# Cross-attention on one core: Wv turned by DMA, a V projection and three Wo slices moved into the first iteration, a stack fill cut in two

## The chip, the core and the metric

The kernel runs on one core of a Trainium2 chip. A core has TensorE (PE in the rows; its weight loads are PEld), VectorE (DVE), ScalarE (ACT), GpSimd (POOL) and SyncE (SP), which issues all DMAs of this kernel from one queue, in order. The metric is device time in microseconds (us), the median over runs.

## The reference

Eight batches; x is 224 x 512 and the context 750 x 512 in each, 16 heads of 32.

```python
q = (x @ Wq.T + bq).reshape(B, Nq, 16, 32).transpose(0, 2, 1, 3)
k = (ctx @ Wk.T + bk).reshape(B, Nk, 16, 32).transpose(0, 2, 1, 3)
v = (ctx @ Wv.T + bv).reshape(B, Nk, 16, 32).transpose(0, 2, 1, 3)
att = softmax(einsum('bhqd,bhkd->bhqk', q, k) / sqrt(32))
out = einsum('bhqk,bhkd->bhqd', att, v).transpose(0, 2, 1, 3).reshape(B, Nq, 512)
out = x + out @ Wo.T + bo
out = (out - mean) / sqrt(var + 1e-5) * gamma + beta
```

## The kernel before

All operands of the large matmuls are split into two f16 parts, a high one (ScalarE) and a low one (VectorE), and a product is three matmuls (high-high, high-low, low-high). Weights and tokens are needed with the 512 input features on the partitions, so they are turned.

**Prologue.** A list of tasks (`prologue`) is run in order by TensorE, each into one of six PSUM banks: four that later hold scores, two that later hold tasks. `("W", "v", 2)` turns 128 rows of Wv by four 128 x 128 transposes; ScalarE and VectorE then write its two parts into `wT`. `("ctxT", i)` and `("xT", i)` turn tokens. `("K", g, half)`, `("Q", g)` and `("V", i)` are projections: K for 128 features and half of the keys, Q for 128 features, V for 125 keys and all features. Their outputs go to `parts` (K, Q) or `v`.

**Iterations.** Each batch is an iteration of 32 steps: four units (of four heads), eight steps each. Step s issues the row scores of step s + 1 (L605), whose row maxima VectorE takes (L911) before the next unit needs them. The unit before is worked on in the same steps: key-major scores (L629), the exponential on ScalarE (L792), sums over keys on GpSimd (L1019 to L1027); the product with V (L645) follows two units behind. Projections are spread over the steps by tables: `OWN` for what this batch still lacks, `NEXT` for the next batch (`("Q", 0)` of the next batch stands at step 24), `OUTPUT` for the output projection of the batch before, steps 18 and 20. Steps 18 and 20 of iteration 0 are empty, as are steps 1 and 9 in it. The tasks use two PSUM banks in turn, and each waits until VectorE has saved the bank's last user.

**Tokens of the next batch** are not turned by TensorE: ScalarE and VectorE split them into `token_parts` (four slots, L776 and L888), and SP turns each 128-token tile with one DMA transpose of both parts (`turn`, L422). `FIRST_READERS` wait for the turns: `("Q", 0)` of the next batch waits for both tiles of xT, `("K", 0, 0)` and `("K", 0, 1)` for their tiles of ctxT.

**SP's order** is written by hand. `fill_stack(g)` copies K and Q parts of one unit into `stacks`, from which the scores are computed; it is 16 DMAs, four for each head (L435, L437, L438), and a head's scores wait for its four. After the loads of the weights, SP waits until the prologue's `("Q", 0)` is saved, fills stack 0, loads half of the next context, x of the next batch and three rows (gamma, beta, bo), fills stack 1 and loads the residual. Iteration 0 then issues, in order: the turns of ctxT 0 and 1, the load of the other context half, the turn of ctxT 2, stack 2, the turns of ctxT 3 to 5, a context load, stack 3, the two turns of xT, a load of x, and, once the next batch's K and Q are saved, stack 0 of the next batch.

Of the kernel before, what the change touches and what calls it, by code (L numbers as in the profile page):

```python
# [12 lines left out]
DMA = 16  # L13


def build(nc, x, ctx_tokens, Wq, bq, Wk, bk, Wv, bv, Wo, bo, gamma, beta, out):
# [31 lines left out]
    AHEAD, INSIDE, BEHIND = range(3)  # L48
    WARM_UP = 8
# [26 lines left out]
    OUTPUT = {18: ("O", 0), 20: ("O", 1)}  # L76
    TASK_BANKS = 2
# [25 lines left out]
    prologue = [("W", "k", 0)] + [("ctxT", i) for i in range(3)] + [("xT", 0), ("xT", 1), ("W", "k", 1), ("W", "k", 2), ("K", 0, 0),  # L103
# [7 lines left out]
    def prologue_inputs(t):  # L111

        if t[0] not in "KQV":
            return []
        found = [("W", "v", f) for f in range(DT)] if t[0] == "V" else [("W", t[0].lower(), t[1])]
        return found + inputs_of(t)

    def tasks_of(b):

        known = isinstance(b, int)  # L120
        found = dict(OWN) if not known or b < B else {}
        found.update(NEXT if not known or b < LAST else {})
        found.update(OUTPUT if not known or b > 0 else {})
        return found
# [28 lines left out]
    def tasks_before(b):  # L153
# [47 lines left out]
    with ExitStack() as stack:  # L201
# [43 lines left out]
        y = sb("y", [P, 2, D])  # L245
        stats = sb("stats", [P, 2, 6])
# [15 lines left out]
        w_loaded = {w: [sem(f"w{w}{f}_loaded") for f in range(DT if w == "k" else 1)] for w in "qkvo"}  # L262
# [143 lines left out]
        def _(sp):  # L406
# [21 lines left out]
            def fill_stack(g):  # L428

                for h in range(HG):  # L430
# [12 lines left out]
            def load_w(w, W):  # L443
                sp.dma_start(w_in[:, "qkvo".index(w)], W.rearrange("(t p) d -> p t d", p=P)).then_inc(w_loaded[w][0], DMA)

            def load_wk_rows(f):
                sp.dma_start(w_in[:, "qkvo".index("k"), f], Wk[P * f:P * f + P]).then_inc(w_loaded["k"][f], DMA)
# [19 lines left out]
            fill_stack(1)  # L467
            load_resid(0)

            def iteration(b, parity):  # L470
# [8 lines left out]

                def wait_split(t):  # L480
# [22 lines left out]
                if has_next(b):  # L503
# [4 lines left out]
                    turn_when_free(("ctxT", 2))  # L508
                if 0 in tasks:
# [31 lines left out]
        def _(pe):  # L541
# [15 lines left out]
            def task(t, n, bank, batch, inside=()):  # L557
# [11 lines left out]
                elif kind == "W":  # L569
                    if t[1] == "k" or t[2] == 0:  # L570
                        pe.wait_ge(w_loaded[t[1]][t[2]], DMA)
                    for k in range(DT):
                        last = nc.tensor.transpose(bank[:, P * k:P * k + P], w_in[:, "qkvo".index(t[1]), t[2], P * k:P * k + P], ident[:])  # L573
# [104 lines left out]
            for n, t in enumerate(prologue):  # L678
# [77 lines left out]
        def _(act):  # L756
# [11 lines left out]
            def token_high(t, batch):  # L768
# [5 lines left out]
                need(act, turned[held], DMA * (batch - back))  # L774
                rows_in = slice(0, padded_rows(t))
# [312 lines left out]
```

## Time and profile before

| | |
|---|---|
| time, median of 3 runs | 647.19 us (646.28 to 649.47) |
| profiled execution | 648.4 us, its span 646.5 us |
| busy share of the span | PE 96%, DVE 73%, POOL 71%, ACT 54% |
| mean granted clock of TensorE | 0.987 |

The span runs from the first to the last instruction of the profiled execution; what its time has beyond the span lies before and after. SP issues DMAs and has no busy share of its own; its queue (SPq) is read from the timeline.

### The profile page before, as it was taken

The page shows a single profiled execution, that of the slowest core. Times are in us where ns is not written, and L with a number is a line of the kernel's source. Part 1 is how long each engine was busy: PE and PEld are TensorE (multiplying, and loading weights), DVE is VectorE, ACT ScalarE, POOL GpSimd, SP SyncE. Part 2 cuts the span into 40 slices and gives each one's busy share as a digit, 9 for nine tenths or more (in the row PEclk, how much of TensorE's full clock was granted, in tenths as well). Part 3 has the DMA queues.
Part 4 walks back from the last instruction along what each step waited for, and adds up shares of the span by engine and source line. Part 5 has one row for each costly group of instructions (what it writes and reads, how often), then busy time and mean ns, then how long its engine had stood idle before and what let it go on. Part 6 is the DMA issues. An engine that isn't in the chain of part 4 may idle for free.

```text
span 646.5 us, 14824 instructions
## 1 busy us (share of the span) xinstructions
PE 621.7 (96%) x5217; PEld 424.2 (66%) x5217; DVE 474.8 (73%) x680; ACT 351.9 (54%) x673; POOL 458.8 (71%) x443
## 2 busy tenths in 40 slices
PE   9989999999999998999999999999999999998994
PEld 7756676766666665666766667666677666764542
DVE  4677677777777586776788677876887768766895
ACT  5424556556565564654655655654565636544661
POOL 9301686875978588585889849775887858777852
PEclk9999999999999998999999999999999999997998
DMA  9367633562256623745037632476237521331020
GB/s 307 115 177 163 145 91 74 128 142 69 64 124 140 127 55 84 155 96 148 25 84 167 143 77 62 100 142 143 54 87 167 98 61 32 88 92 35 2 59 28
DMA packets 96021, 67.09 MB, mean 104 GB/s; under 512 B 69892, under 2 KB 82192, under 8 KB 95952
## 3 DMA queue, kind: packets, MB, share of 16 engines
q1 hardware_dynamic: 95952, 66.16, 42.9%
q8 instruction: 44, 0.72, 0.5%
q14 instruction: 25, 0.20, 0.1%
HBM read 24.52 MB, written 3.67 MB: 44 GB/s over the span
## 4 chain that ended last, share of the span: by engine, by line
PE 81%; DVE 9%; POOL 4%; ACT 2%; issue 2%; POOLq 0%; ACTq 0%; DVEq 0%
PE ps_task L594 37%; PE ps_scores L605 12%; PE ps_task L645 9%; PE ps_scoresT L629 9%; PE ps_task L553 6%; DVE top L911 3%; POOL pair_sums L1019 2%; PE ps_task L671 2%; PE ps_scores L594 2%; DVE attn_sums L918 1%; POOL head_sums L1027 1%; DVE attn_parts L933 1%; ACT probsT L792 1%; POOL head_sums L1024 1%; PE ps_scores L573 1%
## 5 line engine op out<-in xcount | busy, mean ns | idle before, releaser
L792 ACT ACTIVATE probsT<-ps_scoresT 125x448 f32<-125x448 f32 x384 | 204.0, 545 | 198.5 <-PE ps_scoresT L629 183.5
L911 DVE TENSOR_REDUCE top<-ps_scores 112x1 f32<-112x750 f32 x256 | 236.1, 929 | 90.7 <-PE ps_scores L605 89.4
L1019 POOL TENSOR_TENSOR pair_sums<-probsT 125x672 f32<-125x672 f32 x122 | 200.2, 1641 | 116.4 <-ACT probsT L792 107.6
L629 PE MATMUL ps_scoresT<-stacks 100*125 100x224 f16 x768 | 135.5, 261 | 0.9 <-ACT probsT L792 0.4
L594 PE MATMUL ps_task<-wvT,ctxT 128*125 128x512 f16 x564 | 135.3, 379 | 0.9 <-DVE parts L868 0.9
L605 PE MATMUL ps_scores<-stacks 96*112 96x512 f16 (+1 forms) x512 | 127.2, 331 | 6.0 <-DVE top L911 3.7
L594 PE MATMUL ps_task<-ctxT,wkT 128*128 128x375 f16 x708 | 131.9, 325 | 0.1
L629 PEld LDWEIGHTS ps_scoresT<-stacks 100*125 100x125 f16 x768 | 94.1, 137 | 40.3 <-ACT probsT L792 5.5
L1027 POOL TENSOR_TENSOR head_sums<-head_sums,pair_sums 125x224 f32<-125x224 f32 x122 | 90.5, 742 | 9.6
L1024 POOL TENSOR_TENSOR head_sums<-pair_sums 125x224 f32<-125x224 f32 x122 | 89.1, 730 | 10.4
L594 PEld LDWEIGHTS ps_task<-wvT,ctxT 128*125 128x125 f16 x564 | 73.3, 136 | 33.3 <-DVE parts L868 1.1
L594 PEld LDWEIGHTS ps_task<-ctxT,wkT 128*128 128x128 f16 x708 | 68.7, 98 | 33.0 <-issue 2.1
L605 PEld LDWEIGHTS ps_scores<-stacks 96*112 96x112 f16 x512 | 57.4, 130 | 41.4 <-issue 27.3
L645 PE MATMUL ps_task<-probsT,v 125*32 125x224 f32 x1488 | 80.1, 357 | 1.7 <-DVE parts L868 1.7
L645 PEld LDWEIGHTS ps_task<-probsT,v 125*32 125x32 f32 x1488 | 43.8, 110 | 28.9 <-issue 6.2
L873 DVE COPY v<-ps_task 125x512 f32<-125x512 f32 x47 | 32.2, 686 | 39.6 <-PE ps_task L594 39.6
L918 DVE RECIPROCAL attn_sums<-attn_sums 128x112 f32<-128x112 f32 x64 | 49.8, 818 | 1.5 <-ACT attn_sums L800 1.5
L764 ACT ACTIVATE parts<-ps_task,bk 128x375 f16<-128x375 f32 x59 | 33.7, 571 | 28.4 <-PE ps_task L594 25.5
L553 PE MATMUL ps_task<-woT,attn_parts 128*112 128x512 f16 x192 | 47.4, 388 | 0.6 <-DVE attn_parts L933 0.6
L781 ACT ACTIVATE stacks<-ps_scoresT 4x896 f16<-4x896 f32 x32 | 28.9, 904 | 26.1 <-PE ps_scoresT L614 25.6
L594 PE MATMUL ps_task<-xT,wqT 128*128 128x224 f16 x360 | 41.7, 259 | 1.2 <-DVE parts L868 1.2
L888 DVE TENSOR_TENSOR token_parts<-ctx_in,token_parts 128x512 f16<-128x512 f32 (+1 forms) x42 | 28.9, 714 | 18.0 <-ACT token_parts L776 18.0
(100 smaller groups left out, 520.9 us busy)
## 6 DMA issues: line engine op xcount, KB each, us to landing
stacks<-parts SPq DMA_DIRECT2D x256, 60.9 KB, 2.0
ctx_in<-in_ctx SPq DMA_DIRECT2D x8, 768.0 KB, 5.5
stacks<-parts SPq DMA_DIRECT2D x128, 46.9 KB, 2.0
resid<-in_x SPq DMA_DIRECT2D x8, 448.0 KB, 3.9
ctx_in<-in_ctx SPq DMA_DIRECT2D x7, 512.0 KB
out_y<-y SPq DMA_DIRECT2D x16, 224.0 KB, 2.3
x_in<-in_x SPq DMA_DIRECT2D x8, 256.0 KB, 3.1
stacks<-parts SPq DMA_DIRECT2D x128, 14.0 KB, 1.8
```

The lines of the kernel that those rows point to most:

```text
L553: last = nc.tensor.matmul(bank[0:QP, :], attn_parts[:, a, k, QP * q:QP * q + QP], wT["o"][:, c, k, :], start=(k == 0 and (a, c) == (0, 0)) ...
L594: last = nc.tensor.matmul(dst, lhsT, rhs, start=first, stop=(n_mm == 0))
L605: last = nc.tensor.matmul(ps_scores[0:QP, s % RING, keys], stacks[0:STACK_ROWS, g, h, NK + QP * q:NK + QP * q + QP], stacks[0:STACK_ROWS, ...
L629: last = nc.tensor.matmul(ps_scoresT[0:KP, piece % 2, NQ * i:NQ * i + NQ], stacks[:, g, h, KP * k:KP * k + KP], stacks[:, g, h, Qc], start ...
L645: last = nc.tensor.matmul(ps_attn[c:c + DK, 0:NQ], v[of_batch][0:KP, k, P * g + c:P * g + c + DK], probsT[0:KP, g % 2, h, k, :], start=(k ...
L764: nc.scalar.activation(dst, src, ACT.Identity, bias=b16).then_inc(high_saved, 1)
L792: nc.scalar.activation(probsT[0:KP, g % 2, h, 2 * j:2 * j + 2, :].rearrange("p k q -> p (k q)"), ps_scoresT[0:KP, piece % 2, 0:2 * NQ], AC ...
L911: nc.vector.tensor_reduce(top[0:QP, g % 2, HG * q + h:HG * q + h + 1], ps_scores[0:QP, s % RING, 0:NK], AX.X, ALU.max).then_inc(top_ready, 1)
L918: nc.vector.reciprocal(recip[:, cols], recip[:, cols]).then_inc(recip_ready, 1)
L1019: nc.gpsimd.tensor_tensor(pair_sums[0:KP], probsT[0:KP, g % 2, h, 0:3, :], probsT[0:KP, g % 2, h, 3:6, :], ALU.add).then_inc(pair_sums_rea ...
L1024: nc.gpsimd.tensor_tensor(head_sums[0:KP, g % 2, h, :], pair_sums[0:KP, 0], pair_sums[0:KP, 1], ALU.add).then_inc(two_sums_ready, 1)
L1027: nc.gpsimd.tensor_tensor(head_sums[0:KP, g % 2, h, :], head_sums[0:KP, g % 2, h, :], pair_sums[0:KP, 2], ALU.add).then_inc(head_sums_read ...
```

## The change

Wv is no longer turned by TensorE. Behind the prologue's second slice of Wq and behind K(0,1), ScalarE and VectorE split the loaded rows of Wv into `token_parts` (two slices each time), and SP turns each slice with a DMA transpose into `wT`. V(2) and three slices of Wo leave the prologue and become tasks of iteration 0, at steps 1, 9, 18 and 20 (`FIRST`). Wo is loaded in two halves, the second into `y`. SP loads the next context ahead of stack 0, and fills only two heads of stack 1 before iteration 0; the other two heads follow the turn of ctxT 2.

```diff
+    FIRST = {1: ("V", 2), 9: ("W", "o", 1), 18: ("W", "o", 2), 20: ("W", "o", 3)}
...
-                ("K", 0, 1), ("Q", 0), ("W", "q", 2), ("W", "q", 3), ("K", 1, 1), ("W", "v", 0), ("W", "v", 1), ("Q", 1),
-                ("W", "v", 2), ("W", "v", 3), ("K", 3, 0), ("W", "o", 0), ("V", 0), ("W", "o", 1), ("W", "o", 2), ("V", 1),
-                ("W", "o", 3), ("V", 2)]
+                ("K", 0, 0), ("K", 1, 0), ("W", "k", 3), ("ctxT", 3), ("ctxT", 4), ("ctxT", 5), ("K", 2, 0), ("W", "q", 0),
+                ("W", "q", 1), ("K", 0, 1), ("Q", 0), ("W", "q", 2), ("W", "q", 3), ("K", 1, 1), ("Q", 1), ("K", 3, 0),
+                ("W", "o", 0), ("V", 0), ("V", 1)]
+    SPLIT_BEHIND = {("W", "q", 1): (0, 1), ("K", 0, 1): (2, 3)}
...
+        wo_in = (w_in[:, 3, 0:WO_HALF], y[:])
...
-            def fill_stack(g):
+            def fill_stack(g, heads=range(HG)):
...
             load_w("v", Wv)
-            load_w("o", Wo)
+            load_wo_half(0)
+            sp.wait_ge(bias_turned, 1)
+            load_wo_half(1)
+            for f in range(DT):
+                sp.wait_ge(wv_low_saved, f + 1)
+                sp.dma_start_transpose(wT["v"][:, :, :, P * f:P * f + P],
+                                       token_parts[:, f].rearrange("p a d -> p (a d)")).then_inc(wv_turned[f], DMA)
             sp.wait_ge(task_saved, prologue.index(("Q", 0)) + 1)
+            load_ctx(1, 0)
             fill_stack(0)
-            load_ctx(1, 0)
...
             sp.wait_ge(task_saved, prologue.index(("Q", 1)) + 1)
-            fill_stack(1)
             load_resid(0)
+            fill_stack(1, range(HG // 2))
...
-                    sp.wait_ge(task_ready, after(LAST_READERS[t]) if t in LAST_READERS else before)
+                    sp.wait_ge(task_ready, after(LAST_READERS[t]) if t in LAST_READERS else before + moved_readers)
...
                     turn_when_free(("ctxT", 2))
+                if isinstance(b, int) and b == 0:
+                    fill_stack(1, range(HG // 2, HG))
...
+                if t[0] == "V":
+                    for f in range(DT):
+                        pe.wait_ge(wv_turned[f], DMA)
...
+            def weight_high(f):
+                act.wait_ge(w_loaded["v"][0], DMA)
+                nc.scalar.activation(token_parts[:, f, 0], w_in[:, "qkv".index("v"), f], ACT.Copy,
+                                     scale=WSCALE).then_inc(wv_high_saved, 1)
...
+            def weight_low(f):
+                dve.wait_ge(wv_high_saved, f + 1)
+                nc.vector.scalar_tensor_tensor(token_parts[:, f, 1], w_in[:, "qkv".index("v"), f], WSCALE,
+                                               token_parts[:, f, 0], ALU.mult, ALU.subtract).then_inc(wv_low_saved, 1)
```

On SP's queue, at the end of the prologue's weight loads, there stood before (probsT is the region that holds the weights as loaded, in brackets the semaphores waited for):

```order
L444 DMA probsT<-in_L_xattn_Wv 128x4x512
L444 DMA probsT<-in_L_xattn_Wo 128x4x512
L437 DMA stacks<-parts 32x750 [waits task_saved]
L438 DMA stacks<-parts 32x224
L435 DMA stacks<-parts 32x974 x2
```

and now:

```order
L452 DMA probsT<-in_L_xattn_Wv 128x4x512
L456 DMA probsT<-in_L_xattn_Wo 128x2x512
L456 DMA y<-in_L_xattn_Wo 128x2x512 [waits bias_turned]
L476 DMA_TRANSPOSE wvT<-token_parts 128x8x128 [waits wv_low_saved] x4
L418 DMA ctx_in<-in_ctx 128x3x512 [waits task_saved]
L445 DMA stacks<-parts 32x750
L446 DMA stacks<-parts 32x224
L443 DMA stacks<-parts 32x974 x2
```

The first DMA of stack 0 now has four transposes and a context load ahead of it. Between the load of the residual and stack 2, on the same queue, there stood before:

```order
L426 DMA resid<-in_x 112x2x512
L422 DMA_TRANSPOSE ctxT<-token_parts 128x8x128 [waits task_ready,token_low_saved] x2
L410 DMA ctx_in<-in_ctx 128x2x512 [waits token_low_saved]
L414 DMA ctx_in<-in_ctx 110x512
L422 DMA_TRANSPOSE ctxT<-token_parts 128x8x128 [waits task_ready,token_low_saved]
L437 DMA stacks<-parts 32x750 [waits task_saved]
```

and now (the last two heads of stack 1 begin at the last row):

```order
L434 DMA resid<-in_x 112x2x512 [waits task_saved]
L445 DMA stacks<-parts 32x750
L446 DMA stacks<-parts 32x224
L443 DMA stacks<-parts 32x974 x2
L445 DMA stacks<-parts 32x750
L446 DMA stacks<-parts 32x224
L443 DMA stacks<-parts 32x974 x2
L430 DMA_TRANSPOSE ctxT<-token_parts 128x8x128 [waits task_ready,token_low_saved] x2
L418 DMA ctx_in<-in_ctx 128x2x512 [waits token_low_saved]
L422 DMA ctx_in<-in_ctx 110x512
L430 DMA_TRANSPOSE ctxT<-token_parts 128x8x128 [waits task_ready,token_low_saved]
L445 DMA stacks<-parts 32x750
```

Eight of the 16 DMAs of stack 1 have moved behind the three turns. On TensorE, at the end of the prologue and in the first steps, there stood before (the first two rows are V(2), then the scores of steps 0 and 1, K(2,1), the scores of steps 2 and 3, and Q(2)):

```order
L594 MATMUL ps_task<-wvT,ctxT 125x512 [waits task_saved]
L594 MATMUL ps_task<-wvT,ctxT 125x512 x11
L605 MATMUL ps_scores<-stacks 112x512 [waits ones_ready,stacked0_0,pick_ready,task_saved]
L605 MATMUL ps_scores<-stacks 112x238
L605 MATMUL ps_scores<-stacks 112x512
L605 MATMUL ps_scores<-stacks 112x238
L594 MATMUL ps_task<-ctxT,wkT 128x375 [waits task_saved]
L594 MATMUL ps_task<-ctxT,wkT 128x375 x11
L605 MATMUL ps_scores<-stacks 112x512 [waits top_ready,stacked0_1]
L605 MATMUL ps_scores<-stacks 112x238
L605 MATMUL ps_scores<-stacks 112x512 [waits top_ready]
L605 MATMUL ps_scores<-stacks 112x238
```

and now (V(1), the scores, K(2,1), the scores of step 2, V(2)):

```order
L621 MATMUL ps_scores<-wvT,ctxT 125x512 [waits wv1_turned,wv2_turned,wv0_turned,wv3_turned,task_saved]
L621 MATMUL ps_scores<-wvT,ctxT 125x512 x11
L632 MATMUL ps_scores<-stacks 112x512 [waits ones_ready,stacked0_0,pick_ready,task_saved]
L632 MATMUL ps_scores<-stacks 112x238
L632 MATMUL ps_scores<-stacks 112x512
L632 MATMUL ps_scores<-stacks 112x238
L621 MATMUL ps_task<-ctxT,wkT 128x375 [waits task_saved]
L621 MATMUL ps_task<-ctxT,wkT 128x375 x11
L632 MATMUL ps_scores<-stacks 112x512 [waits top_ready,stacked0_1]
L632 MATMUL ps_scores<-stacks 112x238
L621 MATMUL ps_task<-wvT,ctxT 125x512 [waits task_saved]
L621 MATMUL ps_task<-wvT,ctxT 125x512 x11
```

The prologue's last task before the scores is now V(1), and it stands in a scores bank (ps_scores) where V(2) stood in a task bank; V(2) itself has moved between the scores of steps 2 and 3.

## Rows read from the trace of the kernel before

**Rows 1.** The page, part 4: the chain that ended last, by engine.

```profile
PE 81%; DVE 9%; POOL 4%; ACT 2%; issue 2%; POOLq 0%; ACTq 0%; DVEq 0%
```

**Rows 2.** Busy time by stage: stretch, its length, engines, PEclk, DMA share, GB/s.

```profile
22.40:38.35 15.95, 15.95 (x105) 11.79 (x102) 9.40 (x15) 6.36 (x13) 0.21 (x1) 1.00 0.39 108
38.35:86.60 48.25, 44.81 (x319) 30.29 (x318) 36.82 (x50) 23.04 (x44) 20.50 (x20) 1.00 0.69 160
```

**Rows 3.** Timeline of PE, end of the prologue: start, length, what.

```profile
35.32 0.60 PE L573 MATMUL ps_scores<-ident,probsT 128*128 128x128 f32 x4
35.76 2.75 PE L594 MATMUL ps_task<-wvT,ctxT 128*125 128x512 f16 x12
38.35 0.80 PE L605 MATMUL ps_scores<-stacks 96*112 96x512 f16 x4
39.30 2.09 PE L594 MATMUL ps_task<-ctxT,wkT 128*128 128x375 f16 x12
```

**Rows 4.** Timeline of PE in iteration 0; in brackets the idle time before.

```profile
43.26 1.32 PE L594 MATMUL ps_task<-xT,wqT 128*128 128x224 f16 x12 [1.23 <-DVE parts L868]
...
45.55 0.53 PE L605 MATMUL ps_scores<-stacks 96*112 96x512 f16 x2 [0.64 <-DVE top L911]
...
57.52 1.51 PE L594 MATMUL ps_task<-wvT,ctxT 128*125 128x512 f16 x6 [0.87 <-DVE parts L868]
...
86.63 1.31 PE L594 MATMUL ps_task<-xT,wqT 128*128 128x224 f16 x12
```

**Rows 5.** Timeline of SP's queue: start, length of the issue, what.

```profile
6.57 0.51 SPq L444 DMA_DIRECT2D probsT<-in_L_xattn_Wv  x1
...
22.39 0.61 SPq L437 DMA_DIRECT2D stacks<-parts  x1
...
30.64 1.85 SPq L438 DMA_DIRECT2D stacks<-parts  x1
...
50.71 0.85 SPq L410 DMA_DIRECT2D ctx_in<-in_ctx  x1
...
73.43 2.13 SPq L435 DMA_DIRECT2D stacks<-parts  x2
...
80.82 2.67 SPq L422 DMA_TRANSPOSE xT<-token_parts  x2
...
89.63 0.53 SPq L437 DMA_DIRECT2D stacks<-parts  x1
```

**Rows 6.** Waits of SP's queue, 22 to 90 us: total, times, longest.

```profile
SPq L437 <- DVE parts L868: 19.0, 2, 14.0
```

**Rows 7.** DMA transposes of line L422, 40 to 125 us: ns min/median/max.

```profile
L422 SPq DMA_TRANSPOSE ctxT<-token_parts x9: 1241/1256/1937, 47.8 to 118.1; - x9
...
DMA to landing us min/median/max: 2.8/3.4/5.9
```

**Rows 8.** The tile xT, 70 to 100 us: its transposes, first and last start.

```profile
L422 SPq DMA_TRANSPOSE xT<-token_parts x2: 1221/1242/1264, 80.8 to 82.3; - x2
...
DMA to landing us min/median/max: 2.8/3.1/3.3
```

**Rows 9.** DMA issues: KB, median us from issue to landing.

```profile
probsT<-in_L_xattn_Wv SPq DMA_DIRECT2D x1, 1024.0 KB, 12.6
```

**Rows 10.** Timeline of ACT.

```profile
18.44 0.60 ACT L766 ACTIVATE wqT<-ps_task 128x512 f16<-128x512 f32 x1
...
41.90 1.64 ACT L776 CAST token_parts<-ctx_in 128x512 f16<-128x512 f32 x3
...
57.08 1.14 ACT L776 CAST token_parts<-ctx_in 128x512 f16<-128x512 f32 x2 [0.79 <-DMA ctx_in<-in_ctx]
```

**Rows 11.** Timeline of DVE.

```profile
19.22 0.68 DVE L866 SCALAR_TENSOR_TENSOR wqT<-ps_task,wqT 128x512 f16<-128x512 f32 x1
```

**Rows 12.** Busy time around 255 us, columns as in rows 2.

```profile
257.00:258.00 1.00, 1.00 (x4) 0.46 (x3) 0.18 (x1) 0.00 (x0) 0.37 (x1) 0.50 0.07 16
```

**Rows 13.** Timeline of PE at the start of iteration 3.

```profile
254.81 0.87 PE L605 MATMUL ps_scores<-stacks 96*112 96x512 f16 x2 [2.38 <-issue]
```

More of the change, by code:

```diff
@@ L48, in build @@
     AHEAD, INSIDE, BEHIND = range(3)
+    WO_HALF = DT // 2
     WARM_UP = 8
@@ L102, in build @@
     SPLIT_KINDS = ("ctxT", "xT", "K", "Q", "W")
-    prologue = [("W", "k", 0)] + [("ctxT", i) for i in range(3)] + [("xT", 0), ("xT", 1), ("W", "k", 1), ("W", "k", 2), ("K", 0, 0),
[4 rows of a table removed]
+    prologue = [("W", "k", 0), ("ctxT", 0), ("ctxT", 1), ("ctxT", 2), ("xT", 0), ("xT", 1), ("W", "k", 1), ("W", "k", 2),
+                ("K", 0, 0), ("K", 1, 0), ("W", "k", 3), ("ctxT", 3), ("ctxT", 4), ("ctxT", 5), ("K", 2, 0), ("W", "q", 0),
+                ("W", "q", 1), ("K", 0, 1), ("Q", 0), ("W", "q", 2), ("W", "q", 3), ("K", 1, 1), ("Q", 1), ("K", 3, 0),
+                ("W", "o", 0), ("V", 0), ("V", 1)]
+    SPLIT_BEHIND = {("W", "q", 1): (0, 1), ("K", 0, 1): (2, 3)}
+    assert SPLIT_SLOTS == DT
     PRO = len(prologue)
@@ L114, in prologue_inputs @@
             return []
-        found = [("W", "v", f) for f in range(DT)] if t[0] == "V" else [("W", t[0].lower(), t[1])]
+        found = [("W", t[0].lower(), t[1])] if t[0] != "V" else []
         return found + inputs_of(t)
@@ L122, in tasks_of @@
         found.update(NEXT if not known or b < LAST else {})
-        found.update(OUTPUT if not known or b > 0 else {})
+        found.update(OUTPUT if not known or b > 0 else FIRST)
         return found
@@ L426, in load_resid @@
                 sp.dma_start(resid[0:QP], dram(x, b).rearrange("(q p) d -> p q d", p=QP)).then_inc(resid_loaded, DMA)
-            def fill_stack(g):
-                for h in range(HG):
+            def fill_stack(g, heads=range(HG)):
+                for h in heads:
                     rows_of_h = slice(DK * h, DK * h + DK)
@@ L476, in after @@
                     return before + max(tasks[STEP_OF[t]][1] for t in kinds) + 1
+                moved_readers = max((place + 1 for s, (t, place, _) in tasks.items() if isinstance(b, int) and b == 0 and s in FIRST and t[0] == "V"), default=0)
                 def wait_split(t):
@@ L569, in task @@
                 elif kind == "W":
-                    if t[1] == "k" or t[2] == 0:
+                    if t[1] == "o":
+                        pe.wait_ge(wo_loaded[t[2] // WO_HALF], DMA)
+                    elif t[1] == "k" or t[2] == 0:
                         pe.wait_ge(w_loaded[t[1]][t[2]], DMA)
+                    for piece in inside:
+                        scores_keymajor(*piece)
+                    rows_in = wo_in[t[2] // WO_HALF][:, t[2] % WO_HALF] if t[1] == "o" else w_in[:, "qkv".index(t[1]), t[2]]
                     for k in range(DT):
-                        last = nc.tensor.transpose(bank[:, P * k:P * k + P], w_in[:, "qkvo".index(t[1]), t[2], P * k:P * k + P], ident[:])
+                        last = nc.tensor.transpose(bank[:, P * k:P * k + P], rows_in[:, P * k:P * k + P], ident[:])
                 elif kind == "O":
@@ L774, in token_high @@
                 need(act, turned[held], DMA * (batch - back))
+                if isinstance(batch, int) and batch == 1 and back:
+                    act.wait_ge(wv_turned[split_place(t)[1]], DMA)
                 rows_in = slice(0, padded_rows(t))
                 nc.scalar.copy(token_parts[rows_in, split_place(t)[1], 0], tokens_in(t, batch)[rows_in]).then_inc(token_high_saved, 1)
+            def weight_high(f):
+                act.wait_ge(w_loaded["v"][0], DMA)
+                nc.scalar.activation(token_parts[:, f, 0], w_in[:, "qkv".index("v"), f], ACT.Copy,
+                                     scale=WSCALE).then_inc(wv_high_saved, 1)
             def save_maxima(u, g):
@@ L818, in _ @@
                 high_part(t, n, pro_banks[n % PRO_BANKS])
+                for i in SPLIT_BEHIND.get(t, ()):
+                    weight_high(i)
             def iteration(b, parity):
@@ L946, in _ @@
                 splits += t[0] in SPLIT_KINDS
+                for i in SPLIT_BEHIND.get(t, ()):
+                    weight_low(i)
             dve.wait_ge(top_zero, 1)
```

17 lines of the change are left out of this document (12 added, 5 removed), and 1 row of the table prologue.

## The prediction

> **What bounds the kernel now.** I read the chain of waits first: four fifths of it is TensorE [rows 1]. Time is won where TensorE's own work shrinks or its gaps fill. By stage, TensorE is full to the last hundredth in the second half of the prologue and has 48.25 - 44.81 = 3.44 us of gaps between 38.35 and 86.6 us, that is up to step 24 of iteration 0 [rows 2]. The timeline shows the larger gaps: 1.23 and 0.64 us at steps 1 to 3 (Q(2) waits for a saved K, scores wait for a row maximum) and 0.87 us at step 10 [rows 4].
>
> The second view is SP's queue. From 22.39 us, when the prologue's Q(0) is saved, to 80.82 us, the first turn of xT, it issues 80 DMAs: four fills of 16, and 16 others (context, x, rows, residual, six turns) [rows 5]. That is 58.4 us, 0.73 us each. The waits of the queue between 22 and 90 us are two: 14.0 us, which ends at 22.39, and the other 5.0 us, which ends at 89.63, when the next batch's Q(0) has been saved [rows 5, 6]. Between them SP waits for nobody: it is a second engine that is full through the whole of iteration 0, and its last product there, the second turn of xT, is issued at 82.3 us and lands about 3.1 us later, near 85.4 [rows 8]. TensorE reads it in Q(0) at 86.63, without a gap before it [rows 4]. So SP is only 1.2 us ahead of TensorE at this place. That margin is what I take the change by.
>
> **The change on TensorE.** A slice of a weight costs 35.76 - 35.32 = 0.44 us and V(2) 38.35 - 35.76 = 2.59 us [rows 3]. Out of the prologue go four slices of Wv (1.76), three of Wo (1.32) and V(2): 5.67 us. Iteration 0 takes back 1.32 + 2.59 = 3.91. The net removal is 1.76 us, and the rest is won only as far as moved work falls into gaps. V(2) at step 1 stands where Q(2) waited, so the 1.23 and 0.64 us are filled (1.87); the slice at step 9 fills 0.44 of the 0.87 us. The slices at steps 18 and 20 stand in full stretches and win nothing.
>
> Two waits are added. V(0) now needs all four turned slices of Wv (below): before, V(0) began at 38.35 less three V and three Wo slices behind its start, 29.26 us, and with 1.76 us of Wv gone TensorE would reach it at 27.5; the last slice lands near 28 (issued at 24.5, 3.4 us to landing [rows 7]), so 0.4 us is lost. And the scores of step 0 wait for a save they did not wait for: V(1) stands in a scores bank. K(2,1) waited 39.30 - 38.35 = 0.95 us for the save of V(2), with two scores of 0.8 us in that time [rows 3]; now the scores stand behind the save too, 0.8 us more. Sum for TensorE alone: 1.76 + 1.87 + 0.44 - 0.4 - 0.8 = 2.9 us won, and no more than 1.76 + 3.44 = 5.2 if every gap were filled.
>
> **The change on ScalarE and VectorE.** Eight saves from PSUM become eight splits from SBUF at about the same price: a cast of this size takes 1.64 / 3 = 0.55 us on ScalarE and the low part 0.68 on VectorE [rows 10, 11]. TensorE, which is full behind them, hides this as before, and I cost it at nothing, except where it sets the start of the transposes; uncovered it would be eight saves' difference, some tenths of a microsecond. ScalarE is done with Wq's second slice near 19.0 us [rows 10]; Wv was issued at 6.57 and lands 12.6 us later, at 19.2 [rows 5, 9]. A high part (0.55) and a low part (0.68) later, with VectorE free from 19.9 on [rows 11], the first slice is ready at 20.6 us. The other three follow at 0.6 us or so, with K(0,1)'s save between, faster than SP takes them. If the load came late, K(0,1) and Q(0) would be saved late as well, since their saves stand behind it; at 19.2 it delays ScalarE by 0.2 us.
>
> **The change on SP.** Four issues of a transpose at 1.26 us [rows 7], 1.3 with the gap between issues, take SP from 20.6 to 25.8 us. Q(0) is saved by then. The remaining stream, 80 issues up to the first turn of xT, is the same as before in number and kind; only its order differs. It begins at 25.85 instead of 22.39, 3.46 us later, and as it had no waits it cannot catch up. So the second turn of xT is issued at 82.3 + 3.4 = 85.7 and lands at 88.8 (88.5 to 89.0 with the landings of 2.8 to 3.3 us [rows 8]). Before that, nothing on SP is late enough to stop TensorE for longer: halves of stack 1 and the turns of ctxT arrive close to their readers. The load of the other context half is issued at 50.71 + 3.46 - 5.07 (two heads fewer ahead of it, eight issues) = 49.1 and not 50.71, and ScalarE, which had to wait 0.79 us for it at 57.08 [rows 5, 10], now gets it 1.6 us sooner though it would want it 3 us sooner. That costs TensorE up to 1.3 us of its lead, and it reaches Q(0) near 84.5 us (83.7 with the whole lead of 2.9).
>
> There it stands until 88.8: 2.2 us after the 86.63 of before, with some 4.3 us of idle time.
>
> **The clock.** The only gap before of such length, 2.38 us at the start of iteration 3, ended at 254.81, and the granted clock was 0.50 of full speed, the 1.2 GHz level, as far as 258 us [rows 12, 13]. Half of 3.2 us is lost: 1.6 us. The gaps of 0.64 to 1.23 us show no such thing, the mean of that stage is 1.00 [rows 2, 4]. The gap at Q(0) is nearer to the 2.38 us row, so I take 1.6 us; the bounds are nothing and twice that.
>
> **Sum.** 2.2 + 1.6 = 3.8 us longer. Behind step 24 the queue has its 5 us wait again, TensorE's order is the same, and I see no place where the loss comes back. The profiled execution would take 648.4 + 3.8 = 652.2 us; that run lay 1.2 us above the median, and from the median of 647.19 I get 651.0. Bounds: three issues of SP's stream are long (1.85 us where its like takes 0.61, a pair in 2.13 instead of 1.22, a transpose of 1.94 instead of 1.26 [rows 5, 7]), 2.8 us in all, which could be missing or come again. Without them the second turn lands at 88.8 - 2.8 = 86.0, and Q(0) starts 0.6 us earlier than before, with no long gap; with one more long issue and a slow clock twice as long it is 2.2 + 1.2 + 3.2 = 6.6 us later.
>
> **Rivals.** (1) SP keeps pace and TensorE's own sum decides: 2.9 us faster, 644.3, at most 5.2, 642.0. It decides only if the second turn of xT lands by 86.63 - 2.9 = 83.7 us, 1.7 us before it lands now. For it: SP has 5 us to spare directly behind this stream [rows 6]. Against it: the stream of iteration 0 has no wait to give, and 80 issues behind four new ones. The Trainium skill speaks for it: "DMA: Bandwidth & Descriptors", section "Issuing engines are not separate DMA queues", says that the time a sequencer needs to initiate a DMA is usually small relative to the DMA itself. By that rule the four issues cost nothing and the time is this rival's 644.3; the trace does not agree, with 1.26 us of issue in a landing of 3.1 and a queue that is full for 58 us. I give this case 0.12, three quarters of it beyond 0.5% and a quarter within.
> (2) SP is late, but the clock does not fall, or the stream has fewer long issues: between -0.6 and +2.4 us, 646.6 to 649.6, and 649.4 where only the clock term goes. For it: gaps up to 1.23 us did nothing, and the wait may be cut in two by the earlier one at step 10. Chance 0.34.
> (3) More is late: Wv lands later, so that SP's stream starts later by as much, or the turns of ctxT 3 to 5 hold K(0,1) as well (a landing of 5.9 us was seen [rows 7]); over 5 us longer, 652.5. Chance 0.05.
>
> **How the numbers follow.** The main case, SP late and the clock down, has 0.49, with 2.6 to 5.2 us, 649.8 to 652.4. A measurement here can tell some 0.5%, 3.2 us, from no change. Slower by more than that: 0.43 of the main case and rival 3, 0.48. Within: the rest of the main case, rival 2 and a quarter of rival 1, 0.43. Faster: 0.09. The range of 8 in 10 leaves out rival 1 and the far end of rival 3, and reaches from 645.5, between rival 1 and the low end of rival 2, to 653.0.
>
> **What would show it.** Right: four transposes between 20 and 26 us on SP's queue, no wait on it from there to the turns of xT, these issued near 84.3 and 85.7, and a gap of 3 to 5 us in front of the first Q task of the next batch on TensorE, released by the DMA, with a clock of 0.5 behind it; the prologue 5 to 6 us shorter. Wrong: if the xT turns are issued at 82 us or before, the stream was not the fixed thing that I take it for; if there is no gap before Q(0), rival 1 holds; if the gap is there at a clock of 1.0, the second term goes.

## The result, and the profile after

The changed kernel takes 654.09 us (median of 7 runs, 650.9 to 656.82), the kernel before 647.22 on the same occasion (7 runs): a ratio of 1.0099, 95% interval 1.0075 to 1.0122. It is slower by 6.4 us by the ratio (6.9 between the medians), where 3.8 were forecast, and lies 1.1 us above the upper end of the range. The profiled execution took 653.38 us, its span 651.5, at a mean clock of 0.985.

The place that the forecast spoke of is the place where the time goes. TensorE's timeline of the changed kernel, the view of [rows 4] (start, length, what, idle time before it), has:

```profile
30.63 7.05 PE L621 MATMUL ps_scores<-wvT,ctxT 128*125 128x512 f16 x24 [2.19 <-DMA wvT<-token_parts]
38.46 0.84 PE L632 MATMUL ps_scores<-stacks 96*112 96x512 f16 x4 [0.78 <-DVE v L912]
44.30 1.31 PE L621 MATMUL ps_task<-xT,wqT 128*128 128x224 f16 x12
...
57.74 1.51 PE L621 MATMUL ps_task<-wvT,ctxT 128*125 128x512 f16 x6 [0.43 <-DVE parts L907]
...
91.44 1.50 PE L621 MATMUL ps_task<-xT,wqT 128*128 128x224 f16 x12 [3.79 <-DMA xT<-token_parts]
...
109.88 0.36 PE L641 MATMUL ps_scoresT<-ident,top 112*128 112x112 f32 x2
```

The gaps that V(2) and a slice of Wo were to fill are filled: no gap of 1.23 us before Q(2) at 44.30, and 0.43 instead of 0.87 at 57.74. But Q(0) of the next batch begins at 91.44 and not at 86.63, 4.81 us later, after 3.79 us of waiting for xT. The last row is the next turn of row maxima on TensorE, a point that all kernels here pass in the same order of work; before, it began at 103.46. By then 6.42 us are lost: 4.81 at Q(0) and 1.61 behind it. The clock says where the 1.61 went (length, engines' busy times, PEclk, DMA share, GB/s):

```profile
88.00:90.00 2.00, 0.00 (x0) 0.00 (x0) 0.95 (x2) 0.68 (x1) 1.86 (x2) 1.00 0.82 157
...
92.00:94.00 2.00, 2.00 (x18) 1.25 (x20) 0.39 (x1) 0.45 (x1) 0.00 (x0) 0.60 0.32 114
94.00:96.00 2.00, 2.00 (x32) 1.05 (x28) 0.90 (x2) 0.00 (x0) 0.00 (x0) 0.54 0.00 0
96.00:98.00 2.00, 2.00 (x33) 1.35 (x26) 0.41 (x1) 0.22 (x1) 0.00 (x0) 1.00 0.25 62
```

TensorE does nothing from 88 to 90 us, and for some 3 us behind the wait it is at 0.5, the lower of its two levels. The two spans differ by 5.0 us only, since the execution profiled before lost 1.6 us at the start of iteration 3 [rows 12, 13] and this one, after a gap of 2.54 us at the same place, did not; the ratio's 6.4 us agrees with the 6.42.

SP's queue of the changed kernel (start, length of the issue), the view of [rows 5]:

```profile
6.51 0.51 SPq L452 DMA_DIRECT2D probsT<-in_L_xattn_Wv  x1
...
23.18 5.48 SPq L476 DMA_TRANSPOSE wvT<-token_parts  x4
28.71 0.58 SPq L418 DMA_DIRECT2D ctx_in<-in_ctx  x1
...
87.05 2.66 SPq L430 DMA_TRANSPOSE xT<-token_parts  x2
```

The transposes of Wv begin at 23.18 where 20.6 was forecast, the stream behind them at 28.71 (forecast 25.85, before 22.39), the second turn of xT near 88.5. From the stream's first issue to that turn it is 59.8 us, before 82.3 - 22.4 = 59.9: the stream has kept its length and moved by its start. Its start is set by what SP waits for, VectorE's low parts of Wv. VectorE and GpSimd at that time:

```profile
19.37 0.68 DVE L905 SCALAR_TENSOR_TENSOR wqT<-ps_scores,wqT 128x512 f16<-128x512 f32 x1
19.97 0.68 DVE L905 SCALAR_TENSOR_TENSOR wqT<-ps_task,wqT 128x512 f16<-128x512 f32 x1
20.57 3.19 DVE L926 SCALAR_TENSOR_TENSOR token_parts<-probsT,token_parts 128x512 f16<-128x512 f32 x2
23.68 0.59 DVE L907 SCALAR_TENSOR_TENSOR parts<-ps_task,bk,parts 128x375 f16<-128x375 f32 x1
24.20 1.27 DVE L926 SCALAR_TENSOR_TENSOR token_parts<-probsT,token_parts 128x512 f16<-128x512 f32 x2
...
11.92 10.70 POOL L1055 TENSOR_SCALAR_AFFINE_SELECT stacks<-stacks 4x3000 f16<-4x3000 f16 x4
```

```profile
L926 DVE SCALAR_TENSOR_TENSOR token_parts<-probsT,token_parts x4: 673/678/2593, 20.6 to 24.8; 128x512 f16<-128x512 f32 x4
```

The second fence is the low parts' line alone (shortest, median and longest in ns). The first low part begins at 20.57, where the forecast had it at 19.9 (ready at 20.6 less 0.68), and lasts 2.59 us; its three fellows last 0.68. It ends 0.5 us after GpSimd's fourth select, which runs from 19.9 to 22.62 us. Its end does not hang on its start: in experiments 1, 5 and 10 below, the same instruction beside the same select began at 20.73, 19.92 and 20.14, lasted 2.42, 3.24 and 3.02 us, and ended at 23.15 to 23.16 like this one. The low parts of Wq at 19.97, under the same select, last 0.68: one of their two sources is PSUM, while a low part of Wv has both in SBUF.

### The profile page after: what moved, and what is told of

Its sections match the earlier page's. It is cut to its first block, busy times and chain, and to the rows that moved or that the text cites. A ratio compares the mean times of both kernels' runs of the same rounds, so it can differ in the third digit from the quotient of the medians.

```text
span 651.5 us, 14806 instructions
## 1 busy us (share of the span) xinstructions
PE 622.3 (96%) x5201; PEld 423.5 (65%) x5201; DVE 475.2 (73%) x680; ACT 351.2 (54%) x673; POOL 457.9 (70%) x443
## 4 chain that ended last, share of the span: by engine, by line
PE 74%; DVE 10%; POOL 4%; SPq 4%; issue 3%; ACT 2%; DMA 2%; POOLq 0%; ACTq 0%; DVEq 0%
PE ps_task L621 33%; PE ps_scores L632 11%; PE ps_task L672 9%; PE ps_scoresT L656 8%; PE ps_task L575 6%; DVE top L955 3%; POOL pair_sums L1065 2%; PE ps_task L698 2%; PE ps_scores L621 2%; SPq L443 1%; DVE attn_sums L962 1%; POOL head_sums L1073 1%; DVE attn_parts L977 1%; SPq L430 1%; POOL head_sums L1070 1%
## 5 line engine op out<-in xcount | busy, mean ns | idle before, releaser
L621 PE MATMUL ps_task<-wvT,ctxT 128*125 128x512 f16 x552 | 132.5, 379 | 0.4 <-DVE parts L907 0.4
L621 PEld LDWEIGHTS ps_task<-wvT,ctxT 128*125 128x125 f16 x552 | 71.6, 136 | 32.3 <-DVE parts L907 0.6
L621 PE MATMUL ps_task<-xT,wqT 128*128 128x224 f16 x372 | 43.2, 259 | 3.8 <-DMA xT<-token_parts 3.8
```

Source lines behind the costliest of these rows:

```text
L621: last = nc.tensor.matmul(dst, lhsT, rhs, start=first, stop=(n_mm == 0))
```

## The experiments

The theory after the result: SP's stream is a fixed length of issues, started too late by the four transposes and by VectorE's held low part; Q(0) waits for its end and the clock falls behind the wait. The rivals: the moved work on TensorE is what costs; the wait for xT is harmless and another wait would take its place; the clock fell for its own reasons. The first four kernels take the change apart, and the later ones test single terms and repairs. The times are ratios to the kernel before, run on the same chip; where two positions are compared, it is the start of Q(0) (before 86.63) and of the next turn of maxima (before 103.46) in the profiled executions.

**1. Turns of xT ahead of stack 3 in iteration 0** (the rest is the changed kernel).

```diff
+                if first:
+                    for i in range(2):
+                        turn_when_free(("xT", i))
                 if 0 in tasks:
                     fill(3, ("K", 3, 1), ("Q", 3))
```

Expected: 

> The changed kernel, but in iteration 0 SP turns xT ahead of stack 3 instead of behind it; nothing else. Theory (SP's stream is late at the turns of xT): the turns are issued near 77 us instead of 87, TensorE comes to the next batch's Q(0) at 87.4 and goes on, so the 3.8 us of idle time and the 1.6 us of low clock behind it go: about 5.5 us below the changed kernel, 1.000 to 1.003 of before. Rival (the moved V(2) and Wo slices, or the transposes' traffic, cost the time): the ratio stays at 1.007 or above.

Measured: 1.001 (0.9992 to 1.0027). The turns are issued at 77.38, and TensorE reaches Q(0) without a wait:

```profile
77.38 3.46 SPq L430 DMA_TRANSPOSE xT<-token_parts  x2
...
84.85 0.53 PE L636 MATMUL ps_scores<-stacks 96*112 96x512 f16 x2 [0.31 <-DMA stacks<-parts]
...
88.04 1.31 PE L625 MATMUL ps_task<-xT,wqT 128*128 128x224 f16 x12
...
104.87 0.36 PE L645 MATMUL ps_scoresT<-ident,top 112*128 112x112 f32 x2
```

Sixteen issues fewer ahead of one product give back 5.0 of the 6.42 us at the turn of maxima. The wait for xT was not harmless. What is left, 1.4 us, goes with the prologue: V(0) still waits 2.04 us for the turned Wv, and the 24 matmuls behind it still take 7.05 us at a clock that fell to 0.50.

**2. GpSimd's fourth select behind the low parts.** Its result is first read by the scores that begin at 38.46 us.

```diff
+                if g == 3:
+                    pool.wait_ge(wv_low_saved, DT)
                 last = nc.gpsimd.affine_select(out=k_rows, in_=k_rows, compare_op=ALU.not_equal, fill=-MAX_SCALE,
```

Expected: 

> The changed kernel, but GpSimd starts its fourth select on stacks only when the four low parts of Wv are saved; nothing else. Theory (VectorE's first low part took 2.6 us because it stood until GpSimd's select had ended): that low part takes about 0.7 us, the transposes begin 1.9 us sooner, Q(0) starts 1.9 us sooner, still behind a wait and a low clock: ratio near 1.007. Rival (the low part is slow by itself when it begins on freshly loaded rows): it takes 2.6 us again and the time is the same, 1.010.

Measured: 1.0046 (1.0024 to 1.0068), a larger gain than expected (near 1.007). GpSimd, VectorE (all four low parts in ns as above), SP's queue, TensorE, and the clock behind TensorE's wait for stack 1:

```profile
23.37 2.71 POOL L1057 TENSOR_SCALAR_AFFINE_SELECT stacks<-stacks 4x3000 f16<-4x3000 f16 x1 [3.42 <-DVE token_parts L926]
...
20.22 1.28 DVE L926 SCALAR_TENSOR_TENSOR token_parts<-probsT,token_parts 128x512 f16<-128x512 f32 x2
...
L926 DVE SCALAR_TENSOR_TENSOR token_parts<-probsT,token_parts x4: 679/684/684, 20.2 to 22.5; 128x512 f16<-128x512 f32 x4
...
20.93 5.47 SPq L476 DMA_TRANSPOSE wvT<-token_parts  x4
26.45 0.58 SPq L418 DMA_DIRECT2D ctx_in<-in_ctx  x1
...
49.39 0.53 PE L632 MATMUL ps_scores<-stacks 96*112 96x512 f16 x2 [1.84 <-DMA stacks<-parts]
...
89.79 1.31 PE L621 MATMUL ps_task<-xT,wqT 128*128 128x224 f16 x12 [2.31 <-DMA xT<-token_parts]
...
106.61 0.36 PE L641 MATMUL ps_scoresT<-ident,top 112*128 112x112 f32 x2
...
49.39:51.39 2.00, 2.00 (x9) 1.23 (x10) 0.94 (x1) 0.00 (x0) 0.00 (x0) 0.83 0.97 189
51.39:53.39 2.00, 2.00 (x6) 1.12 (x5) 0.00 (x0) 0.00 (x0) 0.00 (x0) 0.50 0.93 154
```

All four low parts take 0.68 us, the transposes start at 20.93, the stream at 26.45, and the wait at V(0) is 0.32. The 2.3 us won at the stream's start come back as 1.65 at Q(0) (89.79 for 91.44), and the clock is 1.00 behind the shorter gap, which is the other 1.6: 3.27 us at the turn of maxima (106.61). That second part is not sure to come: in experiment 11, where SP's order and GpSimd's wait are the same, a gap of 2.22 us at Q(0) brought the clock down, and the turn of maxima came at 108.48. VectorE's instruction was held by the select that ran beside it. SP is now late for stack 1 as well, 1.84 us, with a clock of 0.83 and then 0.50 in the four microseconds behind that wait, which is why TensorE, ahead by 3.9 us at the first scores, comes to Q(0) no sooner than in the changed kernel (87.48 and 87.65).

**3. Wv turned by TensorE again, the rest of the change kept**; and **4. the reverse: the kernel before, with Wv turned by DMA and nothing else.**

```diff
-                ("W", "q", 1), ("K", 0, 1), ("Q", 0), ("W", "q", 2), ("W", "q", 3), ("K", 1, 1), ("Q", 1), ("K", 3, 0),
-                ("W", "o", 0), ("V", 0), ("V", 1)]
-    SPLIT_BEHIND = {("W", "q", 1): (0, 1), ("K", 0, 1): (2, 3)}
+                ("W", "q", 1), ("K", 0, 1), ("Q", 0), ("W", "q", 2), ("W", "q", 3), ("K", 1, 1), ("W", "v", 0), ("W", "v", 1),
+                ("Q", 1), ("W", "v", 2), ("W", "v", 3), ("K", 3, 0), ("W", "o", 0), ("V", 0), ("V", 1)]
+    SPLIT_BEHIND = {}
...
-                sp.dma_start_transpose(wT["v"][:, :, :, P * f:P * f + P],
-                                       token_parts[:, f].rearrange("p a d -> p (a d)")).then_inc(wv_turned[f], DMA)
```

Expected of 3: 

> The changed kernel, but Wv is turned by TensorE in the prologue as before, without the splits and the four DMA transposes; V(2), the Wo slices, the loads and the cut fill stay as changed. Theory (the four transposes on SP's queue, with what delays them, are the loss): SP's stream starts within 1 us of before, the next batch's Q(0) waits under 1 us: 0.997 to 1.001 of before. Rival (the moved tasks or the order of SP's queue are the loss): 1.006 or above.

Measured: 1.0003 (0.9983 to 1.0023). SP's stream starts at 22.72; TensorE comes to Q(0) at 84.91 and waits there for SP, to start where it started before the change (86.63):

```profile
86.65 1.31 PE L617 MATMUL ps_task<-xT,wqT 128*128 128x224 f16 x12 [1.74 <-DMA xT<-token_parts]
```

So the moved V and Wo tasks are worth 1.7 us to TensorE, and SP's queue lets none of it through, even without the transposes.

Expected of 4: 

> The kernel before with one part of the change alone: Wv split on chip and turned by four DMA transposes; V(2), all of Wo and SP's order elsewhere stay as before. Theory: SP's stream starts some 6 us later, Q(0) of the next batch starts near 91 us after a wait of 3 to 4 us at a clock that falls: 1.008 to 1.011, as much as the whole change. Rival (the loss is in the moved tasks): 0.997 to 1.001, since TensorE has 1.8 us less to do.

Measured: 1.0053 (1.0031 to 1.0075), less than expected. SP's queue, then TensorE:

```profile
20.57 7.13 SPq L464 DMA_TRANSPOSE wvT<-token_parts  x4
27.74 0.61 SPq L439 DMA_DIRECT2D stacks<-parts  x1
...
62.82 0.41 PE L635 MATMUL ps_scoresT<-stacks 100*125 100x224 f16 x2 [1.46 <-ACT probsT L808]
...
106.66 0.35 PE L620 MATMUL ps_scoresT<-ident,top 112*128 112x112 f32 x2
```

Here the second low part is held and not the first (3.81 us for the two), so that the transposes begin at 20.57 but the stream only at 27.74. V(0) waits 2.07 us, and the context, loaded later, holds up the exponential, for which TensorE waits 1.46 us; TensorE loses its lead on the way, so that at Q(0), 89.83, there is no wait and no low clock. The 1.6 us that I had added for the clock do not occur. Turning Wv by DMA costs 3.2 us at the turn of maxima by itself, half of the 6.42. The other half comes only with the rest of the change: SP's second turn of xT is issued at 88.5 and not at 86.9, so that Q(0) starts 1.6 us later, and TensorE, which comes to Q(0) two microseconds sooner than here, stands there until the clock falls (1.6 us). Without the transposes the same rest costs nothing (experiment 3).

**5. The wait at Q(0) filled with work that belongs to nothing**: 12 more matmuls into the bank that Q(0) overwrites.

```diff
+                        if isinstance(b, int) and b == 0 and t == ("Q", 0):
+                            for _ in range(12):
+                                nc.tensor.matmul(task_bank(b, s)[:, 0:P], ident[:], ident[:], start=True, stop=True)
```

Expected: 

> The changed kernel with 12 extra matmuls of 128 x 128 in front of the next batch's Q(0) in iteration 0. They write the bank that Q(0) overwrites and compute nothing of the result; they stand where TensorE idled for 3.79 us, and occupy some 2.7 us of it. Theory (an idle TensorE of that length costs a second time, by the clock of 0.54 to 0.60 that was granted behind it in the changed kernel): Q(0) starts at about 91.4 us as before this edit, the clock behind it stays at 1.00, and the pair of scores at the next maxima turn comes 1.6 us earlier; 1.6 us less than the changed kernel, a ratio of 1.007 to 1.008 to the kernel before. Rival (the clock falls with the wait on DMA itself or was not what made the 1.6 us): no difference from the changed kernel, 1.009 to 1.010.

Measured: 1.0065 (1.0045 to 1.0085). TensorE, and the clock in 92 to 96 us:

```profile
30.69 5.37 PE L621 MATMUL ps_scores<-wvT,ctxT 128*125 128x512 f16 x24 [3.10 <-DMA wvT<-token_parts]
...
91.68 1.31 PE L621 MATMUL ps_task<-xT,wqT 128*128 128x224 f16 x12 [1.60 <-DMA xT<-token_parts]
...
108.50 0.36 PE L641 MATMUL ps_scoresT<-ident,top 112*128 112x112 f32 x2
```

```profile
92.00:96.00 4.00, 4.00 (x63) 2.68 (x61) 1.29 (x2) 0.45 (x1) 0.00 (x0) 1.00 0.25 85
```

Q(0) starts 0.24 us later than in the changed kernel, the next turn of maxima 1.38 us earlier: work of no use in a wait saves 1.6 us behind it. The price of the clock was as forecast, and in these two executions it goes with TensorE's idleness, not with the transfer, which is the same in both. The ratios of all runs, 1.0065 and 1.0099, point the same way, but their intervals touch.

**6. Edits 1 and 2 together.**

Expected: 

> The changed kernel with two of the three edits of the kernel with all repairs: GpSimd's fourth select waits for the low parts, and the turns of xT stand ahead of stack 3. The seven loads stay on SP. Theory (each repair removes its own part of SP's lateness): the transposes start at 21 us, the wait for stack 1 of some 1.8 us stays, since 26 issues of SP still start 4 us later than before the change, Q(0) starts near 87.3 without a gap and with a clock of 1.00: 0.7 us later than before the change, ratio 1.000 to 1.002. So the loads on ScalarE's queue are worth some 2.5 us of the 2.8 by which the kernel with all repairs stands ahead of this one. Rival (the loads moved did nothing, the two other repairs made the whole gain): 0.996, as with all repairs.

Measured: 0.9985 (0.9962 to 1.0008), somewhat better than expected. In the profiled execution (648.4 us, 1.2 above the median) TensorE waited 1.06 us for context tiles at 8.23 us, the first low part began at 21.61 (20.22 in experiment 2) and the transposes at 22.32; Q(0) is at 87.82 without a wait, and stack 1 is waited for, 2.01 us.

**7. Experiment 3 with the turns of xT ahead.**

Expected: 

> Wv turned by TensorE as before, the rest of the change kept, and the two turns of xT issued ahead of stack 3 in iteration 0. Theory (SP's queue, not TensorE, decided at Q(0) in the kernel with Wv on TensorE, where Q(0) waited 1.74 us for xT and started at 86.65): with the turns 16 issues earlier the wait goes, Q(0) starts near 84.9, and 1.7 us are won: ratio 0.996 to 0.998. Rival (stack 3, now two issues later, or stack 0 of the next batch is waited for instead, as 1.4 us were in the kernel with xT ahead): 0.999 to 1.001.

Measured: 0.9964 (0.9945 to 0.9984). No wait at Q(0), and none for a stack:

```profile
85.17 1.31 PE L621 MATMUL ps_task<-xT,wqT 128*128 128x224 f16 x12
...
102.00 0.36 PE L641 MATMUL ps_scoresT<-ident,top 112*128 112x112 f32 x2
```

**8. All repairs, Wv still turned by DMA**: edits 1 and 2, and seven loads on ScalarE's queue. **9. The same loads moved in experiment 7. 10. The loads alone moved in the changed kernel.**

```diff
-            load_ctx(1, 0)
             fill_stack(0)
-            load_x(1)
...
+            act.wait_ge(task_saved, prologue.index(("Q", 0)) + 1)
+            tokens = dram(ctx_tokens, 1)
+            act.dma_start(ctx_in[:, 0:HALF_TILES], tokens[0:P * HALF_TILES].rearrange("(k p) d -> p k d", p=P)).then_inc(ctx_loaded[0], DMA)
...
+            act.dma_start(resid[0:QP], dram(x, 0).rearrange("(q p) d -> p q d", p=QP)).then_inc(resid_loaded, DMA)
```

Expected of 8: 

> The changed kernel, Wv turned by DMA, with three edits: GpSimd's fourth select waits until the four low parts are written, the turns of xT stand ahead of stack 3 in iteration 0, and seven loads (half of the next context, two of x, the three rows, the residual) are issued from ScalarE's queue behind its last part of the prologue instead of SP's. Theory (the order and the fullness of SP's queue are all that stood against the change): the transposes start at 20.9 us, the stream of SP is some 4 us shorter, stack 1 and Q(0) wait for nobody, Q(0) starts at 84 to 85.5, and 1.3 to 2 us are won: ratio 0.997 to 0.998. Rival (ScalarE is held by the issuing of loads, or the loads share the DMA engines with the stack fills at the same time, so that the stacks land late): 1.000 to 1.003.

Expected of 9: 

> Wv turned by TensorE, the rest of the change kept, the turns of xT ahead of stack 3, and the seven loads on ScalarE's queue behind its last part of the prologue. Theory (with no transposes of Wv on SP and the loads off it, TensorE alone decides in iteration 0): Q(0) starts at 84 to 85, no wait for stacks; ratio 0.995 to 0.997, a little better than the same without the loads moved, if stack 3 was late there. Rival (SP had room enough with the turns ahead; moving the loads gives nothing or costs ScalarE some tenths): the same ratio as the kernel with xT ahead alone, 0.997, or 0.001 more.

Expected of 10: 

> The changed kernel with one of the three edits: seven loads go to ScalarE's queue, nothing else is undone. Theory (SP's stream is a sum of issues): GpSimd's select still holds the first low part, the transposes start at 23.2, the stream is 4 us shorter (seven issues of 0.43 to 0.58, and their gaps), the second turn of xT is issued at 84.5 to 85 and lands at 87.5 to 88; TensorE, which has waited 2.2 us for V(0), reaches Q(0) near 86.5 to 87 and waits about 1 us there, without a fall of the clock: Q(0) starts at 87.5 to 88, ratio 1.001 to 1.003. Rival (the transposes' late start costs the same wherever the stream's length lies): 1.006 or more.

Measured: 8 gives 0.9961 (0.9940 to 0.9982), 645.01 us; 9 gives 0.9961 (0.9945 to 0.9977), 645.1 us; 10 gives 1.0017 (1.0001 to 1.0033), inside its expectation. TensorE in 8:

```profile
28.57 5.37 PE L620 MATMUL ps_scores<-wvT,ctxT 128*125 128x512 f16 x24 [0.27 <-DMA wvT<-token_parts]
...
38.05 0.53 PE L631 MATMUL ps_scores<-stacks 96*112 96x512 f16 x2 [0.57 <-DMA stacks<-parts]
...
84.53 1.31 PE L620 MATMUL ps_task<-xT,wqT 128*128 128x224 f16 x12
...
101.36 0.36 PE L640 MATMUL ps_scoresT<-ident,top 112*128 112x112 f32 x2
```

The turn of maxima is 2.1 us earlier than before the change, and every wait that SP made is down to 0.6 us. This kernel and 7 and 9 are faster than the kernel before by 0.4%, and than the changed kernel by some 1.4%. Between 7 and 9 nothing can be told: with the turns ahead SP had room. Between 8 and 9 neither: taking Wv off TensorE is worth nothing measurable even where SP has room for it. The seven loads by themselves bring the changed kernel from 1.0099 to 1.0017; beside the two other repairs (8 against 6) the medians are 2.2 us apart, but the intervals of the two ratios overlap.

The profiled execution of 10 took 655.75 us, the longest of its 14 (median 649.54), so its trace shows a mishap and not the median. One of the four transposes of Wv landed 6.4 us after its issue (the other three 3.4), V(0) waited 6.04 us, and TensorE was at the low clock behind it:

```profile
L476 SPq DMA_TRANSPOSE wvT<-token_parts x4: 1318/1330/1370, 23.2 to 27.4; - x4
...
DMA to landing us min/median/max: 3.4/3.4/6.4
```

The loads on the other queue begin at 27.85, while the last transpose is issued, and the DMA share from 26 to 34 us is 0.98 to 1.11. That the loads delayed it is likely, but only argued; in 8, where the transposes are over two microseconds earlier, all landed within 3.4.

**11. What holds VectorE: a memset in the select's old place.** GpSimd writes the same 4 x 3000 elements and reads nothing; the select follows behind the low parts.

```diff
+                if g == 3:
+                    nc.gpsimd.memset(k_rows, 0.0).then_inc(pick_zero, 1)
+                    pool.wait_ge(pick_zero, 2)
+                    pool.wait_ge(wv_low_saved, DT)
```

Expected: 

> The changed kernel with GpSimd's fourth select behind the low parts, and in its old place a memset of the same 4 x 3000 elements of stacks, which the select then overwrites with what it wrote before. The memset writes and reads nothing. Theory A (what holds VectorE is a GpSimd instruction that reads SBUF while VectorE has two sources there): the first low part takes 0.6 to 0.7 us although a GpSimd instruction of 2.5 us runs beside it, and the transposes start at 21 us. Theory B (any GpSimd instruction on SBUF holds it): the first low part takes 2 us or more, until the memset ends near 22.5, and the transposes start at 22.6 or later.

Measured (one run, 650.34 us): theory A. GpSimd, then VectorE:

```profile
19.90 2.59 POOL L1056 MEMSET stacks<- 4x3000 f16 x1
...
20.12 1.29 DVE L926 SCALAR_TENSOR_TENSOR token_parts<-probsT,token_parts 128x512 f16<-128x512 f32 x2 [0.18 <-ACT token_parts L812]
...
L926 DVE SCALAR_TENSOR_TENSOR token_parts<-probsT,token_parts x4: 678/682/692, 20.1 to 22.4; 128x512 f16<-128x512 f32 x4
```

The low parts take 0.68 to 0.69 us with the memset beside them, and the transposes start at 20.84. A memset and a select differ in more than in what they read, so this run alone does not show that the reading is what holds VectorE.

## Why the prediction was wrong: right place, one term too small

**The step that failed** is the start of the transposes: "A high part (0.55) and a low part (0.68) later, with VectorE free from 19.9 on [rows 11], the first slice is ready at 20.6 us". VectorE was free at 20.57, and not unhindered: the low part took 2.59 us, and the first slice was ready at 23.18, 2.58 us late. The late start adds nothing to that, since the end came with the select's. I had priced the instruction by a row of the same operation and shape [rows 11] without asking where its sources lie, and what GpSimd did meanwhile. The page "SBUF — State Buffer" of the Trainium skill, section "Who interferes with whom", says that a VectorE instruction with two inputs in SBUF contends with a GpSimd instruction that reads SBUF and not with one that only writes it. The runs agree: 2.59 us beside the select, 0.68 without it (experiment 2) and 0.68 to 0.69 beside a memset (experiment 11).

**SP.** From this start on the forecast was close. Four transposes and the way to the stream's first issue took 5.53 us (forecast 5.25), the stream 59.8 (59.85), and from the second turn of xT to Q(0) it was 3.0 (landing 3.1). So Q(0) is late by 2.2 + 2.58 + 0.28 - 0.25 = 4.8 us, 2.6 of them new. Rival 1, by which the four issues cost nothing, is contradicted: 1.3 us of issue in a landing of 3.3, and all of it handed on to the end of the stream. The time is where rival 3 (0.05) had it, and SP's stream did start later, but for neither of its reasons: Wv landed 11.1 us after its issue, sooner than before (12.6), and K(0,1) of the next batch waited for no turn. A slip without weight: SP's queue had a third wait between 22 and 90 us before the change, 0.4 us for a save, which the prediction left out where it says that SP waits for nobody.

**TensorE.** It reaches Q(0) at 91.44 - 3.79 = 87.65, where I had 84.5. The 3.15 us are: 0.9 at V(0), which TensorE reaches at 28.44 instead of 27.5 (0.75 of it at the very start, eight matmuls in 1.59 us for 1.06 and four in 1.06 for 0.80, at a clock of 1.00; why is open); 1.8 in V(0)'s wait, 2.19 us for 0.4, which is the same late start of the transposes; 1.7 behind that wait, at a clock of 0.5, which I had not thought of (24 matmuls in 7.05 us, 5.37 at full clock in experiment 5); less 1.3 behind the prologue, where the later context load was to take up to 1.3 of a lead that TensorE no longer had. The scores' wait for V(1), 0.78, and the filled gaps came as forecast. None of this counted in the time: SP was later still.

**The clock.** 1.6 us forecast, 1.61 found, and 1.6 taken away by filling the wait. The size was right. Its source row says little about when it comes, though: of 22 waits near that row's 2.38 us 12 had it (the last section); the wait here was longer, 3.79 us.

**Sum.** 4.81 + 1.61 = 6.42, forecast 2.2 + 1.6 = 3.8. With the held low part taken away (experiment 2) the time is 1.0046, 3.0 us, near the forecast; that is luck in part, since it is made of 3.2 us at Q(0) and no fall of the clock there, instead of 2.2 and 1.6. And the sentence that nothing on SP is late enough to stop TensorE before Q(0) did not hold there: stack 1 was waited for, 1.84 us, with a fall of the clock.

In nine of the twelve kernels the place of the next turn of maxima in one execution tells the ratio to within 0.2%: 6.42 us later for 1.0099, 3.15 for 1.0046, 3.20 for 1.0053, 5.04 for 1.0065, 1.41 for 1.001, 0.02 for 1.0003, 1.46 earlier for 0.9964, 1.47 for 0.9961, 2.10 for 0.9961. To that accuracy nothing behind iteration 0 gives back or adds to what is decided there. (Experiments 6 and 11 are off by 0.3%, the latter with a single run; experiment 10, whose profiled execution was its longest, by 0.9%.)

## What to carry to other kernels

A queue that issues without waits is an engine like the others: sum its issues from its first free moment to the product that another engine waits for, and look for what else could issue them, or for an order that puts that product first; here 16 issues of order were worth 5 us, and Wv off TensorE nothing. A price taken from a row of the same operation holds only if the sources lie in the same memories and the neighbours do the same; for an instruction on VectorE with both sources in SBUF look at what GpSimd reads beside it. Before work is taken off the bounding engine and given to a queue, see what the queue's next wait is: work given to a full queue comes back as a wait, and a wait of two to four microseconds on TensorE may, as here, cost another 1.6 by the clock behind it.

## What the runs showed of the hardware that had not been expected

VectorE and GpSimd held each other in both directions, and the one that began first went on. VectorE's low parts (shortest, median, longest) of experiments 5 and 4, and GpSimd's four selects of experiment 4:

```profile
L929 DVE SCALAR_TENSOR_TENSOR token_parts<-probsT,token_parts x4: 673/678/3237, 19.9 to 24.8; 128x512 f16<-128x512 f32 x4
...
L905 DVE SCALAR_TENSOR_TENSOR token_parts<-probsT,token_parts x4: 678/688/3200, 19.9 to 24.7; 128x512 f16<-128x512 f32 x4
...
11.92 11.20 POOL L1034 TENSOR_SCALAR_AFFINE_SELECT stacks<-stacks 4x3000 f16<-4x3000 f16 x4
```

In experiment 5 the fourth select begins at 19.91 us (22.62 less 2.71) and the first low part at 19.92: the low part lasts 3.24 us and the select its usual 2.71. In experiment 4 the first low part began at 19.85 and took 0.68; the four selects then took 11.20 us instead of 10.70, and the second low part, held until the select's end, 3.20.

The length of a wait alone did not tell whether the clock fell. The profiled executions of the thirteen kernels have, from 20 us on, 22 waits of TensorE between 1.84 and 3.10 us. Behind 12 of them the clock was at 0.5 for some microseconds (2.04 at V(0) in experiment 1, 1.84 for stack 1 in experiment 2, 2.22 at Q(0) in experiment 11), behind 10 it stayed at 1.00 (2.07 at V(0) in experiment 4, 2.31 at Q(0) in experiment 2, 3.10 at V(0) in experiment 5). Of eight waits of 1.46 to 1.74 us four left it at 1.00; four others (1.50 to 1.55 us, near 610 us in experiments 1, 3, 8 and 11) had it at 0.50 two microseconds later. Two of 3.79 and 6.04 us brought it down. What decides below 3.1 us is left open; for a forecast such a wait has two prices, here 1.6 us apart.
